# Aggregation stage of a two-layer graph network: for two of an item's four edge groups alpha is carried by VectorE's one-hots, for the other two ScalarE scales the messages

## What is computed

```python
a = a @ aW3 + ab3
alpha = jax.nn.softmax(a, axis=0)                  # over all edges, per head
alpha_mean = alpha.mean(axis=1, keepdims=True)     # one number per edge
agg = jax.ops.segment_sum(msg * alpha_mean, dst, num_segments=N)
out = node_features + agg @ W_out
```

## Time and profile before

| what | value |
|---|---|
| median of three runs | 3500.36 us |
| span of the profiled execution | 3499.8 us |
| TensorE matmul / weight load busy | 2791.7 us (80%) / 1977.5 us (57%) |
| VectorE / ScalarE / GpSimd busy | 2528.0 us (72%) / 2041.3 us (58%) / 2085.4 us (60%) |
| aggregation, first `pick` to last add | from 3108.59 to about 3438.1 us of the span |
| of it, the looped items 8 to 247 | from 3120.70 to 3431.49 us |
| mean granted TensorE clock | 0.962 of 2.4 GHz |

### The profile page before, as it was taken

How to read it: one execution, slowest core, us unless ns; L and a number is a source line. 1 busy time by engine, 2 the same in 40 slices (tenths; PEclk the granted TensorE clock), 3 DMA queues, 4 the chain that set the end, 5 groups by cost and what they waited for, 6 DMA issues and landing times. The chain is left out here.

```text
span 3499.8 us, 76247 instructions
## 1 busy us (share of the span) xinstructions
PE 2791.7 (80%) x17156; PEld 1977.5 (57%) x17380; DVE 2528.0 (72%) x4445; ACT 2041.3 (58%) x4527; POOL 2085.4 (60%) x2160
## 2 busy tenths in 40 slices
PE   1577777777777777744799999999999999958885
PEld 0355555555555555532466666666666666647774
DVE  5699999999999999996345555555554555567776
ACT  6355555555555555545355555555555555568885
POOL 0177777777777777732777777777777777500001
PEclk9899999999999999978899999999999999989997
DMA  2555444554444444413777777777777777647662
GB/s 71 172 143 145 142 142 141 142 144 144 142 139 141 143 141 143 141 34 106 206 218 222 218 218 221 220 218 221 217 222 220 220 220 218 190 132 202 202 202 82
DMA packets 391734, 595.68 MB, mean 170 GB/s; under 512 B 73317, under 2 KB 237855, under 8 KB 391682
## 3 DMA queue, kind: packets, MB, share of 16 engines
q0 software_dynamic: 98304, 268.57, 27.1%
q1 hardware_dynamic: 242626, 247.55, 25.4%
q10 hardware_dynamic: 50752, 78.99, 6.6%
HBM read 501.15 MB, written 93.68 MB: 170 GB/s over the span
## 5 line engine op out<-in xcount | busy, mean ns | idle before, releaser
L1194 POOL DMA_INDIRECT l_G<-rows_d,l_sidx x1024 | 1002.5, 979 | 363.1 <-issue 276.3
L807 POOL DMA_INDIRECT l_G<-rows_d,l_sidx x1024 | 1014.0, 990 | 330.5 <-issue 305.0
L1322 ACT ACTIVATE l_h<-l_H,l_cols 128x512 f32<-128x512 f32 x512 | 350.7, 685 | 557.3 <-PE l_H L1229 540.5
L875 PE MATMUL l_accp<-l_we,l_ohe 128*128 128x256 f32 x2048 | 486.3, 380 | 0.0
L831 PE MATMUL l_A<-ident,l_G 128*128 128x128 f32 x1024 | 172.8, 293 | 380.6 <-DVE l_oht L978 323.0
L1386 DVE TENSOR_TENSOR big<-l_SC,l_b 128x512 f32<-128x512 f32 x256 | 177.1, 692 | 387.9 <-PE l_SC L1258 387.9
L875 PEld LDWEIGHTS l_accp<-l_we,l_ohe 128*128 128x128 f32 x2048 | 371.1, 191 | 40.1
L831 PEld LDWEIGHTS l_A<-ident,l_G 128*128 128x128 f32 x1024 | 111.2, 144 | 482.0 <-issue 243.5
L1258 PEld LDWEIGHTS l_SC<-big,l_h 128*128 128x128 f32 x2048 | 263.6, 191 | 146.8 <-issue 146.8
L1548 PE MATMUL ag_accp<-ag_msg,ag_pick 128*128 128x128 f32 x2048 | 286.5, 288 | 73.7 <-ACT ag_msg L1532 32.9
L903 ACT ACTIVATE l_qe<-l_A 128x512 f32<-128x512 f32 x256 | 153.3, 599 | 325.8 <-PE l_A L834 209.7
(11 more groups left out here) (182 smaller groups left out, 5755.4 us busy)
## 6 DMA issues: line engine op xcount, KB each, us to landing
msg_d<-l_msg ACTq DMA_DIRECT2D x256, 256.0 KB, 2.2
ag_msg<-msg_d SPq DMA_DIRECT2D x256, 256.0 KB, 2.9
l_G<-rows_d,l_sidx POOLq DMA_INDIRECT x2048, 3.3
l_lo<-mark_d SPq DMA_DIRECT2D x256, 128.0 KB, 3.0
l_lo<-code_d SPq DMA_DIRECT2D x256, 128.0 KB
l_in<-in_ea_dram SPq DMA_DIRECT2D x512, 64.0 KB
l_fd<-dst_d SPq DMA_DIRECT2D x256, 96.0 KB, 3.4
l_pd<-dst_d SPq DMA_DIRECT2D x256, 96.0 KB
```

Of the source, the lines that this page charges most:

```text
L807: nc.gpsimd.indirect_dma_start(out=G[:, s, j, :], out_offset=None, in_=rows_d[0][:, :], in_offset=bass.IndirectOffsetOnAxis(ap=sidx[:, hal ...
L875: last = nc.tensor.matmul(accp[b][:, 0:2 * C], oh_e[:, b, j, :], we_t[:, b, j, :], start=(j == 0), stop=(j == TJ - 1), skip_group_check=True)
L1194: nc.gpsimd.indirect_dma_start(out=G[:, s, j, :], out_offset=None, in_=rows_d[1][:, :], in_offset=bass.IndirectOffsetOnAxis(ap=sidx[:, hal ...
L1322: nc.scalar.activation(out_t[:, s % 2, :], in_p[:, :], ACT.Silu, bias=cols[:, col:col + 1]).then_inc(ready, 1)
```

## The change

The four one-hot matrices of an item are split. `PLAIN` = 2 of them still come from one `tensor_tensor`, now over 128x256. The other two are written by one `tensor_scalar` each (128x128), with two per-partition scalars: is-equal against the local destination, then times alpha. Their messages are not scaled by anyone. ScalarE scales groups 0 and 1 of every item, the line 1597 scaling with its wait for the load is gone, and the counts that TensorE waits for become 2 and 3 per item.

```diff
-            OWN = [TJ - 1 + s % 2 for s in range(U)]
-            SHARED = [sum(OWN[0:s + 1]) for s in range(U)]
-            PICKED = [sum(1 + TJ - n for n in OWN[0:s + 1]) for s in range(U)]
+            PLAIN = TJ // 2
+            PICKS = 1 + TJ - PLAIN
...
-                            for j in range(TJ - OWN[s], TJ):
+                            for j in range(PLAIN):
...
-                            pe.wait_ge(shared, lp * SHARED[-1] + SHARED[s])
-                            pe.wait_ge(pick_ready, lp * PICKED[-1] + PICKED[s])
+                            pe.wait_ge(shared, PLAIN * (i + 1))
+                            pe.wait_ge(pick_ready, PICKS * (i + 1))
...
-                            nc.vector.tensor_tensor(pick[:, b, :, :], iota_row[:, :].unsqueeze(1).to_broadcast([P, TJ, P]),
-                                                    local[:, bass.ds(i * TJ, TJ)].unsqueeze(2).to_broadcast([P, TJ, P]),
+                            nc.vector.tensor_tensor(pick[:, b, 0:PLAIN, :], iota_row[:, :].unsqueeze(1).to_broadcast([P, PLAIN, P]),
+                                                    local[:, bass.ds(i * TJ, PLAIN)].unsqueeze(2).to_broadcast([P, PLAIN, P]),
                                                     ALU.is_equal).then_inc(pick_ready, 1)
-                            if OWN[s] == TJ:
-                                return
-                            dve.wait_ge(ld[s], 16 * (lp + 1))
-                            mine = msg_t[:, s, 0, :]
-                            nc.vector.tensor_scalar(mine, mine, al[:, bass.ds(i * TJ, 1)], None,
-                                                    ALU.mult).then_inc(pick_ready, 1)
+                            for j in range(PLAIN, TJ):
+                                nc.vector.tensor_scalar(pick[:, b, j, :], iota_row[:, :], local[:, bass.ds(i * TJ + j, 1)],
+                                                        al[:, bass.ds(i * TJ + j, 1)], ALU.is_equal, ALU.mult).then_inc(pick_ready, 1)
```

## The result

The changed kernel takes 3558.14 us (median of four runs, 3556.98 to 3565.47) against 3500.85 us: ratio 1.0164, 95% interval 1.015 to 1.0179. It is 57 us slower. The forecast was 3551 us. The profiled execution is the longest of the four (3565.47 us).

What follows compares the result with a forecast made beforehand. The prediction took VectorE's instruction issue to bound the loop: a lap of 10.38 us loses 0.78 and gains 2.40, +48.6 us over 30 laps; with +2.2 for unrolled items, 3551 us, range 3529 to 3595.

Steps and rivals of the forecast that it cites:

- What bounds the kernel: In the looped aggregation items, the issue of VectorE's instructions is the bound, not its arithmetic: 1.295 us an item against 0.90.
- Removed, 9.60 us a lap left: Four VectorE scalings fewer per lap of eight items save 0.78 us of issue: 10.38 becomes 9.60 us.
- Added, 16 x 0.15 = 2.40: Sixteen new `tensor_scalar` a lap on VectorE, each priced at the line 1597 scaling's 0.15 us of issue: 2.40 us.
- bounds 0.11 and 0.24: Lowest and highest issue cost in us of each new `tensor_scalar` on VectorE: 1.76 to 3.84 us a lap.
- `pick` halved, worth nothing: VectorE's engine saves 0.27 us an item on the one-hots, but the sequencer issues one instruction as before: no gain.
- VectorE's own work 1.04 us an item: VectorE's engine part after the change, 1.04 us an item, stays below the sequencer's interval of 1.39.
- ScalarE relieved, worth nothing: ScalarE runs 16 activations a lap instead of 28, 3.6 us less, on an engine five items ahead: no gain.
- loads and TensorE follow: Same 256 KB loads and eight matmuls an item, only slower; TensorE, busy 1.12 us an item, keeps up.
- Unrolled items, at most +2.2 us: The 16 items outside the loop run at the engine's pace, 1.04 instead of 0.90 us: +2.2 us at most.
- Rival 1: ScalarE sets the aggregation loop's pace, so relieving it gains 62 us: about 3438 us; 3 in 100.
- Rival 2: VectorE's arithmetic, not its sequencer, sets the pace: +0.03 to +0.14 us an item, 3508 to 3537 us; 5 in 100.
- 3 (twice the rate): On VectorE only elements count and the new form runs two a cycle: -59 us, 3441 us; 2 in 100.

## Why the prediction was right, step by step

- *What bounds the kernel*: held. Less arithmetic (64 us of busy time) changed nothing; less issue brought 62 and 66 us.
- *Removed, 9.60 us a lap left*: held. The kernel without scalings had 9.58 us. That it agrees so closely is in part luck. The second and fourth step fell by 0.15 and the sixth by 0.24, as priced; the eighth fell by 0.37 instead of 0.24, and the first grew by 0.12, for a reason that stays open. The two misses cancel.
- *Added, 16 x 0.15 = 2.40*: this term was mis-sized. It measured 12.27 - 9.58 = 2.69, or 0.168 for each instruction. I argued that an address and a wait value in a 65 ns block are as much work as two addresses. The block is 99 ns, and the plain steps grew from 1.09 to 1.455: 0.18 for each instruction. The step with the branch grew by less, from the 1.61 us that it has without any scaling to 1.88. There the `pick` starts 0.52 us after the add, in the kernel without scalings 0.61, so 0.09 us of the saving lie ahead of the new instructions, at the branch; why stays open. In all, the 30 laps cost 57.4 us more (368.19 against 310.79) where I had 48.6, and the unrolled items 0.8 us less than my figure: 58.8 us in the stage where I had 50.8. The median of the runs lies 7 us above the forecast. The bounds 0.11 and 0.24 held.
- *`pick` halved, worth nothing*: held (310.80 us in the earlier trace rows, 310.96 with the halved one). *VectorE's own work 1.04 us an item*: held, 1.046.
- *ScalarE relieved, worth nothing; loads and TensorE follow*: held; predicted 175 GB/s and a busy time of 57% of before, measured 172 and 62%.
- *Unrolled items, at most +2.2 us*: the ends took 0.75 and 0.62 us longer.
- *Rival 1 (ScalarE sets the pace)*: refuted; with four activations a lap more the kernel got faster. *Rival 2 (arithmetic) and 3 (twice the rate)*: refuted by the halved `pick` and by the old form with more arithmetic and less time. The Trainium skill ("VectorE: DVE Perf Modes", The perf-mode tier table) gives that rate for instructions of 2048 elements. The new form ran here at 128 elements only, 0.255 us from start to start, so no run here tells its rate from a fixed part. *Rival 4 (hidden)*: refuted.

## What to carry to other kernels

In a hardware loop of small instructions, ask what the sequencer does between them: where "issue" gaps stand before the instructions of an engine that is not full, the price of one more instruction may be its addresses, as here, and not its elements. Count who is how many items ahead before believing a releaser; here the names of the waits pointed at several engines and the counts at one. And before work is spread over more instructions on such an engine, look for register work to take off it: leaving away the check of one loaded value was worth 66 us, and the best sharing of the scalings tried here 20. It is safe only where the kernel itself wrote the values.

## What the runs showed of the hardware

- While the sequencer set the pace, a `tensor_scalar` with two addresses that depend on the loop cost 0.16 to 0.20 us on VectorE, one with a single address 0.15, one with constant addresses 0.02 to 0.035, though each runs 0.28 to 0.34 us in the engine.
- A register load from SBUF took 0.30 us on VectorE's sequencer, one of four values 1.02 us, and nothing was issued meanwhile.
- The check of a loaded value's bounds cost 0.26 to 0.29 us an item in the changed kernel, almost as much as the load: the lap fell from 12.27 to 10.21, the plain steps from 1.455 to 1.17 us.
